# Down product of an expert's tokens past 64 in 32-wide parts, and a new order of TensorE's work in the expert loop

## What is computed

```python
logits = x @ Wr
probs = jax.nn.softmax(logits, axis=-1)
top_w, top_i = jax.lax.top_k(probs, K)                  # K = 6 of E = 64 experts
top_w = top_w / jnp.sum(top_w, axis=-1, keepdims=True)
gate = jnp.zeros((N, E), dtype=x.dtype).at[jnp.arange(N)[:, None], top_i].set(top_w)
for e in range(E):
    routed = routed + _swiglu_ffn(x, Wg[e], Wu[e], Wd[e]) * gate[:, e:e + 1]
out = (shared + routed + x).reshape(B, S, d)
```

## Time and profile before

| | us |
|---|---|
| time, median of 3 runs | 1010.12 |
| lowest, highest | 1009.44, 1018.12 |
| span of the profiled execution | 1017.5 |
| PE busy | 895.9 (88%) |
| DVE, POOL, ACT busy | 548.1, 268.2, 256.0 |

### The profile page before, as it was taken

The page is one execution under the profiler, slowest core; times in us unless marked ns, Lnnn a source line. Parts: engine busy times, 40 slices in busy tenths (PEclk is TensorE's granted clock), DMA queues, the critical chain, the costliest instruction groups (busy, mean ns, idle before and its releaser), DMA issues. The chain is left out here.

```text
span 1017.5 us, 20833 instructions
## 1 busy us (share of the span) xinstructions
PE 895.9 (88%) x7497; PEld 589.3 (58%) x7497; DVE 548.1 (54%) x1623; ACT 256.0 (25%) x573; POOL 268.2 (26%) x265
## 2 busy tenths in 40 slices
PE   1599998897878298999999999999999989999991
PEld 1355555564544196676556566766676765656660
DVE  7997987978798986323324333334233332333216
ACT  2111101121130132333322322333233322322331
POOL 4543321334300102222222222222222322222211
PEclk9699999999989789999999999999999999999996
DMA  8856454565428951889979999999988999999976
GB/s 276 287 207 207 158 186 171 207 207 208 166 63 279 373 206 57 319 303 367 405 290 334 359 383 413 390 387 361 405 307 332 353 400 398 365 374 366 402 289 262
DMA packets 76929, 300.68 MB, mean 296 GB/s; under 512 B 13730, under 2 KB 14119, under 8 KB 58548
## 3 DMA queue, kind: packets, MB, share of 16 engines
q1 hardware_dynamic: 57256, 254.21, 65.9%
q0 software_dynamic: 17280, 38.48, 10.5%
q10 hardware_dynamic: 2252, 6.06, 1.7%
HBM read 290.26 MB, written 26.62 MB: 311 GB/s over the span
## 5 line engine op out<-in xcount | busy, mean ns | idle before, releaser
L1202 DVE TENSOR_TENSOR arena<-arena 128x288 f32 (+1 forms) x640 | 236.3, 449 | 37.8 <-remote 24.5
L1826 PE MATMUL bank<-arena,low 128*64 128x256 f32 x2048 | 241.6, 383 | 2.0 <-issue 2.0
L1667 PE MATMUL bank<-arena,multi 128*64 128x256 f32 x1296 | 162.0, 400 | 44.0 <-DVE arena L1202 32.6
L1826 PEld LDWEIGHTS bank<-arena,low 128*64 128x64 f32 x2048 | 141.0, 137 | 75.6 <-issue 12.4
L1851 PE MATMUL bank<-arena,low 128*64 128x256 f32 x1392 | 161.6, 379 | 1.1 <-ACT low L980 1.1
L1667 PEld LDWEIGHTS bank<-arena,multi 128*64 128x64 f32 x1296 | 99.5, 144 | 102.2 <-issue 44.2
L743 POOL DMA_INDIRECT low<-xr_d,idx x64 | 90.2, 1409 | 238.7 <-DVE place L1433 177.6
L747 POOL DMA_INDIRECT y_d<-low,place x64 | 68.5, 1070 | 262.3 <-ACT low L987 181.8
L1851 PEld LDWEIGHTS bank<-arena,low 128*64 128x64 f32 x1392 | 101.3, 137 | 50.3 <-ACT low L980 1.3
L987 ACT ACTIVATE low<-bank,gcol 64x256 f32<-64x256 f32 x174 | 82.1, 472 | 105.0 <-PE bank L1851 103.9
L687 POOL DMA_INDIRECT arena<-xn_d,ssel x79 | 90.3, 1143 | 38.2 <-issue 21.8
(11 more groups left out here) (214 smaller groups left out, 710.9 us busy)
## 6 DMA issues: line engine op xcount, KB each, us to landing
arena<-in_L_ffn_Wg_dram SPq DMA_DIRECT2D x64, 1024.0 KB
arena<-in_L_ffn_Wu_dram SPq DMA_DIRECT2D x64, 1024.0 KB
arena<-in_L_ffn_Wd_dram SPq DMA_DIRECT2D x64, 1024.0 KB
arena<-in_edge_attr_dram SPq DMA_DIRECT2D x88, 256.0 KB
arena<-y_d SPq DMA_DIRECT2D x5, 1250.0 KB, 6.8
sums_d<-arena ACTq DMA_DIRECT2D x18, 256.0 KB, 3.2
arena<-sums_d SPq DMA_DIRECT2D x4, 896.0 KB
arena<-in_L_mix_W_qkv_dram SPq DMA_DIRECT2D x2, 1024.0 KB, 18.1
```

Of the source, the lines that this page charges most:

```text
L1202: return dve.tensor_tensor(prod[:, buf, 0:n, EXT * p:EXT * p + EXT], x1[b][:, 0:n, bass.ds(i1, EXT)], x2[b][:, 0:n, bass.ds(i2, EXT)], ALU ...
L1667: ins = pe.matmul(bank[2 * b + c // 2][64 * h:64 * h + 64, 256 * (c % 2):256 * (c % 2) + 256], pair[:, pairs, i, :], prod[:, buf, i, 256 * ...
L1826: ins = pe.matmul(out_bank[64 * h:64 * h + 64, w * HF:(w + 1) * HF], xgT[:, b, k, 64 * o:64 * o + 64], gu[:, slot, w, k, h * HF:(h + 1) * HF],
```

## The change

The down product of an expert's tokens past 64 is done per part of 32 tokens (`part_down`), with four column groups: group q holds output columns 128q to 128q + 127, so an instruction has 128 columns. It goes into the bank that held the expert's gate and up. VectorE, not ScalarE, scales it by the gate weights, in eight instructions of 32x128 per expert, with the weights copied to the right partitions in eight small copies. ScalarE copies both transposed h at once, a bank of 512 columns, for every expert. On TensorE the order of a step becomes: second h and first h transposes, transposes of x, lookup, `part_down` of e - 1, `gate_and_up_part` of e, gate, up, `down(0)`, shared piece. The register load of every eighth step moves in front of the parts, one register takes the place of two (a value over UPTO = 127 means both parts), and a new semaphore s_part, counted in every step by VectorE after a small memset, is waited for by TensorE (before it reuses the bank) and by GpSimd (before the scatter). VectorE waits for the scatter of e - 2 before the second product.

The core of the diff:

```diff
@@ ScalarE
             for e in range(NX + 1):
+                if e >= 1:
+                    act.wait_ge(s_hTp, e)
+                    act.copy(hT[:, :, :].rearrange("p o n -> p (o n)"), bank[2][:, :]).then_inc(s_hT, 1)
...
-                    with act.If(0 < ov):
-                        hold(act, "act", o_y, ov)
-                        scale(1, bank[OV], (e - 1) % PLACES, (e - 1) % 2).then_inc(o_ys, 1)
@@ VectorE
+            def overflow_rest(e):
+                i, b = e % PLACES, e % 2
+                w = dve.snap(over[e % 16], min_val=0, max_val=UPTO + BOTH)
+                if e >= 2:
+                    dve.wait_ge(s_scat[b], 16 * (e // 2))
+                with dve.If(0 < w):
+                    hold(dve, "dve", o_sg, w & UPTO)
+                    dve.tensor_tensor(hO.rearrange("p b (c j) -> p b j c", c=2), sgO.rearrange("p (b j c) -> p b j c", b=2, c=2),
+                                      bank[OV][CAP:CAP2, :].rearrange("p (b j c) -> p b j c", b=2, c=2), ALU.mult).then_inc(o_h, 1)
+                    for r in range(2):
+                        row = CAP + PART * r
+                        for q in range(4):
+                            ins = dve.tensor_copy(gpart[PART * q:PART * q + PART, r:r + 1], gall[row:row + PART, i:i + 1])
+                    ins.then_inc(o_gate, 1)
+                    hold(dve, "dve", o_gate, w & UPTO)
+                    hold(dve, "dve", o_y, w & UPTO)
+                    for r in range(2):
+                        row = CAP + PART * r
+                        for q in range(4):
+                            at = PART * q
+                            dve.tensor_scalar(yy[row:row + PART, b, 128 * q:128 * q + 128],
+                                              bank[GU_BANK[b]][at:at + PART, 128 * r:128 * r + 128], gpart[at:at + PART, r:r + 1], None, ALU.mult)
+                dve.memset(marks[:, e:e + 1], 0.0).then_inc(s_part, 1)
@@ TensorE
+            def part_down(r, slot, out_bank):
+                for k in range(DC):
+                    a = 128 * r + 64 * (k % 2) + PART * (k // 2)
+                    for q in range(4):
+                        ins = pe.matmul(out_bank[PART * q:PART * q + PART, 128 * r:128 * r + 128], hT[:, 1, a:a + PART],
+                                        dn[:, slot, k, 128 * q:128 * q + 128], start=(k == 0), stop=(k == DC - 1), skip_group_check=True)
+                return ins
...
+            def overflow_parts(e, slot):
+                w = pe.snap(over[e % 16], min_val=0, max_val=UPTO + BOTH)
+                with pe.If(0 < w):
+                    hold(pe, "pe", o_h, w & UPTO)
+                    with pe.If(UPTO < w):
+                        gate_and_up_part(1, e % 2, slot, bank[OV])
+                    gate_and_up_part(0, e % 2, slot, bank[OV]).then_inc(o_U, 1)
...
+                if e >= 1:
+                    ov = pe.snap(over[(e - 1) % 16], min_val=0, max_val=UPTO + BOTH)
+                    pe.wait_ge(s_h, e)
+                    if e >= 2:
+                        pe.wait_ge(s_hT, e - 1)
+                    with pe.If(0 < ov):
+                        hold(pe, "pe", o_h, (ov & UPTO) + 1)
+                        part_transpose()
+                    h_transpose(0, bank[2]).then_inc(s_hTp, 1)
...
                 if e >= 1:
-                    ov = pe.snap(over[(e - 1) % 16], min_val=0, max_val=NX)
-                    pe.wait_ge(s_h, e)
-                    h_transpose(0, bank[2]).then_inc(s_hTp, 1)
+                    pe.wait_ge(s_wd[last], 16 * last_fill)
+                    with pe.If(0 < ov):
+                        pe.wait_ge(s_hT, e)
+                        with pe.If(UPTO < ov):
+                            part_down(1, last, bank[GU_BANK[(e - 1) % 2]])
+                        part_down(0, last, bank[GU_BANK[(e - 1) % 2]]).then_inc(o_y, 1)
                 if e < NX:
...
+                    if e >= 2:
+                        pe.wait_ge(s_part, e - 1)
                     pe.wait_ge(s_wg[slot], 16 * fill)
+                    if e > 0:
+                        if e % PLACES == 0:
+                            pe.load(over[e % 16:e % 16 + PLACES], vrow[:, e:e + PLACES])
+                        pe.wait_ge(s_wu[slot], 16 * fill)
+                        overflow_parts(e, slot)
                     gate_or_up(0, e % 2, slot, 0, bank[GU_BANK[e % 2]])
-                if e >= 1:
-                    with pe.If(0 < ov):
-                        hold(pe, "pe", o_h, ov)
-                        part_transpose(bank[OV]).then_inc(o_hTp, 1)
-                if e < NX:
                     pe.wait_ge(s_wu[slot], 16 * fill)
                     gate_or_up(0, e % 2, slot, 1, bank[GU_BANK[e % 2]]).then_inc(s_U, 1)
...
-                    with pe.If(0 < ov):
-                        hold(pe, "pe", o_hT, ov)
-                        down(1, last, bank[OV]).then_inc(o_y, 1)
```

More of the change, by code:

```diff
@@ L989, in scale, with overflow_silu @@
                 return ins
-            act.sem_inc(o_ys, 1)
+            def overflow_silu(e):
+                w = act.snap(over[e % 16], min_val=0, max_val=UPTO + BOTH)
+                with act.If(0 < w):
+                    hold(act, "act", o_U, w & UPTO)
+                    act.activation(sgO, bank[OV][0:CAP, :], ACT.Silu).then_inc(o_sg, 1)
             act.wait_ge(s_xrd, 32)
@@ L1009, in _ @@
                         act.wait_ge(s_scat[(e - 1) % 2], 16 * ((e - 1) // 2))
-                    with act.If(0 < ov):
-                        hold(act, "act", o_y, ov)
-                        scale(1, bank[OV], (e - 1) % PLACES, (e - 1) % 2).then_inc(o_ys, 1)
                     act.wait_ge(s_y, e)
                     scale(0, bank[5], (e - 1) % PLACES, (e - 1) % 2).then_inc(s_ys, 1)
[L1015 to L1018, removed]
-                if e < NX:
[L1020 to L1023, removed]
+                if e == 0:
+                    act.wait_ge(s_flags, 1)
+                    act.load(over[0:PLACES], vrow[:, 0:PLACES])
+                    overflow_silu(0)
                 if AFTER.get(e, ("", 0))[0] == "up":
@@ L1457, in _ @@
             then(dve, dve.tensor_tensor_scan(upto_f, over_f, over_f, 0.0, ALU.add, ALU.bypass))
-            dve.tensor_tensor(vrow[:, 0:NX], over_f, upto_f, ALU.mult)
-            dve.tensor_scalar(vrow2[:, :], counts, float(CAP + PART), None, ALU.is_gt)
+            then(dve, dve.tensor_tensor(upto_f, over_f, upto_f, ALU.mult))
+            then(dve, dve.tensor_scalar(over_f, counts, float(CAP + PART), float(BOTH), ALU.is_gt, ALU.mult))
+            dve.tensor_tensor(vrow[:, 0:NX], upto_f, over_f, ALU.add)
             more = extra.rearrange("p (e j) -> p e j", j=4)
@@ L1927, in _ @@
                     down(0, last, bank[5]).then_inc(s_y, 1)
-                if e < NX:
-                    w = pe.snap(over[e % 16], min_val=0, max_val=NX)
-                    w2 = pe.snap(over2[e % 16], min_val=0, max_val=1)
-                    with pe.If(0 < w2):
-                        hold(pe, "pe", o_ys, w)
-                        gate_and_up_part(1, e % 2, slot, bank[OV])
-                    with pe.If(0 < w):
-                        hold(pe, "pe", o_ys, w)
-                        gate_and_up_part(0, e % 2, slot, bank[OV]).then_inc(o_U, 1)
+                if e == 0:
+                    pe.wait_ge(s_flags, 1)
+                    for at in (bank[OV], bank[2]):
+                        pe.matmul(at[:, HF:2 * HF], ident[:, :], iota[:, 0:HF], start=True, stop=True)
+                    pe.load(over[0:PLACES], vrow[:, 0:PLACES])
+                    overflow_parts(0, slot)
                 if e in AFTER:
```

52 lines of the change are left out of this document (20 added, 32 removed).

## The result

The changed kernel takes **1134.07 us** (median of 4 runs, 1127.96 to 1146.79), the kernel before 1010.67 beside it: ratio **1.1203 [1.1167, 1.1239]**, slower by some 120 us where I had forecast 12. The highest of the four times was a slow run, and the ratio leaves it out. The direction held, the size is off by ten. The profiled execution took 1127.96 us, with a span of 1126.2 and a mean granted clock of 0.942 (before: 0.961).

The account below looks back on a forecast made before the run. TensorE's instruction stream was taken to bound the expert loop. The terms -16.8 + 11.3 + 7 + 3.5 + 3 + 4 gave +12 us: 1030 from 1018.1, or 1022 on the median of 1010.1; eight in ten, 1002 to 1038.

Parts of the forecast that it names:

- What bounds the kernel: Expert loop: TensorE's instruction stream bounds it end to end, so a microsecond added or removed arrives at the kernel's end.
- The new products: New down part on TensorE: eight rounds of four 128-column products at 0.11 us each, 0.95 us for one part.
- rival 3: New down part: rounds do not shorten but keep 0.22 us, +25 us on top, 1047 us; chance 0.07.
- The transposes: Transposes at the head of an overflowing expert's iteration on TensorE: 0.34 us, in place of 0.53.
- The wait for the second h: TensorE after down, before the second h's transposes, waits for L1492: 0.75 us, 15 times, +11.3 us.
- The wait for hT: First down part waits for ScalarE's 128x512 copy: 0.3 us, 23 times, +7 us.
- the sum's 0.2 for semaphore, branch and first load: Last piece, 0.2 us, of the 1.27 us chain from the h transposes' start to the first down part.
- VectorE's scaling: Eight scalings per overflowing expert, 0.29 us each, make the next mult 0.3 to 0.7 late in 8 cases: +3.5 us.
- The register load: TensorE's sequencer: the load, now before the parts with little queued, costs 7 x 0.4 = +3 us.
- the direct saving: TensorE's work alone: shorter down parts and moved transposes, together -16.8 us.
- the price of skipped bodies: TensorE's branches over the longer bodies that non-overflowing experts skip: between 0 and 20 us, taken as +4.
- rival 4: Code fetch on TensorE: skipped bodies of twice the length miss more often, +15 us more, 1037 us; chance 0.10.

Follow-up runs that it names:

- one_part: The changed kernel without the second 32-token part of gate and up and of the down product (tokens past 96 left out): 990.79 us, ratio 0.9926.

## Why the prediction was wrong

**What bounds the kernel**: right. TensorE's stream sets the end; SyncE still waits for its down product (470.9 us in the loop), and what TensorE lost came out at the end (120.6 us in the loop, 123 between the medians).

**The new products**: right. The timeline of the changed kernel around an overflowing expert:

```profile
797.37 0.46 PE L1868 MATMUL bank<-ident,low 64*128 64x64 f32 x4
797.76 0.44 PE L1844 MATMUL bank<-ident,low 128*128 128x128 f32 x2
798.03 0.60 PE L1839 MATMUL bank<-ident,low 128*128 128x128 f32 x4
798.47 0.27 PE L1834 MATMUL bank<-low 125*128 125x7 bf16 x5
799.26 1.08 PE L1875 MATMUL bank<-arena,low 128*32 128x128 f32 x32 [0.52 <-ACT low L1008]
800.53 1.93 PE L1860 MATMUL bank<-arena,low 128*32 128x256 f32 x32 [0.19 <-issue]
```

The part takes 1.08 us with the end of its last product, which is 0.27 long: 0.81 for seven steps, 0.12 per round, against 0.11 predicted and 0.22 as the other end; rival 3 is out. The Trainium skill ("TensorE: Matmul & The Clock Gate", Back-to-back issue gap), whose 81 ns per product would have made 2.6 us of it, does not hold for these products in four column groups: here it is 34 ns a pair. The transposes take 0.39 (797.37 to 797.76), against 0.34.

**The wait for the second h**: right in place and number (15 times), a little small: 8.8 us against 11.3. **The wait for hT**: 22 times, 9.1 us against 7; one_part shows that some 6 of them are the branch over the second body behind the semaphore. The branch is in the sum's 0.2 for semaphore, branch and first load, but was not seen as the larger part of the wait. **VectorE's scaling**: in the groups by line of VectorE

```profile
L1502 DVE TENSOR_SCALAR low<-bank,gpart 32x128 f32<-32x128 f32 x184 | 64.2, 349 | 68.8 <-PE bank L1875 66.4
```

a scaling takes 0.35 us, not 0.29, and eight 2.8. The wait that it was to cause (h of the first part, late) is L1844's 1.7 us, of the 3.5 predicted. **The register load** and **the direct saving** can't be seen singly; one_part checks the rest as a sum: some +9 measured, +8 predicted. The near agreement is of the sum and in part luck: single terms were off by up to 2.5 us, and one_part has only 3.0 us of the hT term's 7.

**The step that failed** is "Between 0 and 20 us; I take +4, as about half of today's gaps again", the price of skipped bodies, and with it rival 4, which had the mechanism and gave it 15. It measured 79 us more of idle time named issue in the loop (85.6 against 6.2), and 26 us of slower products behind the stalls: some 105, and one_part takes 111 away. Two errors in it. I took the price from the gaps and branches of the kernel before and scaled it as if the cost went with the length of skipped code. It doesn't: 128 instructions in the stretch in front of gate cost next to nothing (one_part), 192 cost some 4% and 256 some 12%. The records of the code queue make this slope plausible: code comes in pieces of 256 instructions, and a miss takes up to 4.7 us. In one_part a piece comes every 8.4 us of the loop, in the kernel before every 7.8, in the changed one every 7.1 with its stalls, and without them it would need one every 6. A skip of 256 always leaves the piece that it starts in, one of 128 half the time. By the same reading a skip that lands shortly before the end of a piece brings the stall for the next one in the middle of the products. The kernel before stood at the foot of that slope, and its 3.9 us branch was a sample of what is on it. The Trainium skill has a rule for it that I had not weighed ("Runtime: NRT & Kernel Launch", Instruction fetch mechanics): code is fetched in blocks of 16 KiB ahead of a stream that runs straight on, and a taken branch whose target is not in the two blocks at hand has to wait for its block to be fetched. The trace agrees on the blocks and on the wait: packets of 16,384 bytes only, and the end of every long branch 2.3 to 2.9 us after the start of one. The same section gives TensorE's instruction memory as 128 KiB, 2048 instructions; if all of it were kept filled ahead, a skip of 256 would hardly ever miss, and the 13 long branches at L1916 speak against that much code being at hand. The page has no price for the wait; the runs give up to some 4.7 us, 5.5 once. The second error: I left out that a stall of this length takes the clock down, though the profile has the granted clock for every stretch.

I had also put a top to the unknown cost (20 us) without a row that excludes more: what bounds it is the longest branch seen, 3.9 us, times the 41 experts that skip, 160 us. A range made from that would have held the result.

**What stays open.** The runs show that never entered code makes the stalls, that nearly all of them end with the arrival of one piece of code, at a branch or within the products behind it, that one long stretch costs more than two short ones, and that a third of the cost goes with the weights' traffic. When a piece is asked for (as the stream enters the one ahead of it, as the spacing of the packets suggests) is my reading, and how many are kept at hand was not measured by itself. No version here beats the kernel before and computes all of it: one_part is 0.7% faster for 16 us of products left out.

## What to carry to other kernels

Code that is skipped is not free on an engine that is the bound: count the instructions between the last one entered and the next, for the path that is taken most often, and keep rare bodies short and apart, with long products between them. A body unrolled for each of 64 experts and entered by 6 of them cost seven times as much for being there as for being run (111 us against 16). And where a cost has never been seen at the size that a change gives it, take its bound from the worst single event times the number of chances, not from the sum so far.

## What the runs showed of the hardware

A branch over skipped code on TensorE takes 0.21 us at the median; at the end of a stretch of up to 256 instructions 13 of 64 took over 0.5 us, up to 5.48. Nearly half of the stalled time (36 of 81 us) was not at a branch but in the middle of the products behind it. TensorE's code came in single packets of 16 KB, 0.97 us each, and execution went on 2.4 us after a packet's start; for the long branches the start came up to 2.5 us after the branch, 3.1 once. Never entered code, with no other change but masked wait numbers (under 1% in the versions without a body), cost 2.8%, 6.0% and 11.8% of the time (64 and 128 instructions in a stretch of their own, 128 added to one of 130). After a stall of 4.5 us the granted clock was 0.50 for 4 us of full work. Eight rounds of four 128-column float32 products in four column groups took 0.81 us from the first to the last start, with a weight load of 32 columns for each.
